# A selective-scan kernel: the state laid out as pairs of states by 64 channels, instead of one state by 128 channels

## The reference, cut to what matters

```python
dt = softplus(dt_low @ dt_proj_w.T + dt_proj_b)        # 256 channels d
def step(h, inputs):                                   # h: 256 channels x 16 states
    dt_t, B_t, C_t, u_t = inputs
    dA = jnp.exp(dt_t[:, :, None] * A)
    h = dA * h + (dt_t * u_t)[:, :, None] * B_t[:, None, :]
    y = jnp.einsum('bdn,bn->bd', h, C_t)
    return (h, y)
```

## Time and profile before

| | |
|---|---|
| median of 3 runs | 1285.89 us |
| lowest and highest | 1283.64, 1287.60 us |
| the profiled execution | 1284.42 us |
| its span in the trace | 1282.6 us |
| mean granted PE clock | 0.936 of full speed |
| share of the span busy: PE, DVE, ACT, POOL | 84%, 90%, 64%, 86% |
| moved by DMA | 116.78 MB |

### The profile page before, as it was taken

How to read it: one execution, slowest core, us unless ns; L and a number is a source line. 1 busy time by engine, 2 the same in 40 slices (tenths; PEclk the granted TensorE clock), 3 DMA queues, 4 the chain that set the end, 5 groups by cost and what they waited for, 6 DMA issues and landing times.

```text
span 1282.6 us, 13041 instructions
## 1 busy us (share of the span) xinstructions
PE 1072.5 (84%) x3642; PEld 613.6 (48%) x3642; DVE 1150.1 (90%) x1341; ACT 819.0 (64%) x1532; POOL 1106.9 (86%) x747
## 2 busy tenths in 40 slices
PE   5678878888888887888888889888878878888797
PEld 4334545545545544544455455445445445454344
DVE  1299999999999999999999999999999999999782
ACT  2476766766666667757667666666667676576543
POOL 4199898898898898998988988988988989989663
PEclk8699998998998999999999989989999999998898
DMA  6222221221222312212222212222122132222561
GB/s 162 76 76 76 81 100 65 98 100 58 99 76 86 101 57 105 100 57 98 87 77 80 101 57 99 93 71 99 59 102 101 57 105 100 74 99 87 181 206 37
DMA packets 64538, 116.78 MB, mean 91 GB/s; under 512 B 34218, under 2 KB 47954, under 8 KB 64466
## 3 DMA queue, kind: packets, MB, share of 16 engines
q1 hardware_dynamic: 64466, 115.96, 26.9%
HBM read 108.47 MB, written 7.47 MB: 90 GB/s over the span
## 4 chain that ended last, share of the span: by engine, by line
POOL 27%; DVE 24%; issue 21%; PE 19%; ACT 7%; POOLq 0%; DMA 0%; DVEq 0%; SPq 0%; ACTq 0%
POOL SCAN L414 15%; DVE SCAN L984 15%; PE Yp L711 7%; POOL SCAN L426 6%; DVE SCAN L939 5%; PE PP L740 2%; PE PP L862 2%; PE PP L790 2%; PE PP L842 2%; POOL XN L451 2%; PE PP L835 1%; DVE GATES L968 1%; ACT SGZ L599 1%; POOL GATES L419 1%; POOL XN L442 1%
## 5 line engine op out<-in xcount | busy, mean ns | idle before, releaser
L984 DVE TENSOR_TENSOR_SCAN SCAN<-DA,CAR,SCAN 128x384 f32<-128x384 f32 x768 | 729.8, 1000 | 39.3 <-POOL SCAN L426 35.7
L414 POOL TENSOR_TENSOR SCAN<-SCAN,CS 128x768 f32<-128x768 f32 x384 | 692.3, 1817 | 23.1 <-DVE SCAN L984 18.9
L711 PE MATMUL Yp<-SCAN,IDENT 128*128 128x384 f32 x1536 | 592.6, 511 | 101.1 <-POOL SCAN L414 93.0
L491 ACT ACTIVATE DA<-UDT,A 128x384 f32<-128x384 f32 x768 | 441.6, 581 | 365.3 <-DVE SCAN L984 362.5
L711 PEld LDWEIGHTS Yp<-SCAN,IDENT 128*128 128x128 f32 x1536 | 288.8, 198 | 309.8 <-POOL SCAN L414 147.3
L939 DVE TENSOR_TENSOR SCAN<-UDT,BB 128x768 f32<-128x768 f32 x288 | 268.4, 932 | 11.1 <-PE BB L693 9.2
L426 POOL TENSOR_TENSOR SCAN<-UDT,BS 128x768 f32<-128x768 f32 x96 | 174.4, 1817 | 0.0
L862 PE MATMUL PP<-XN,WT 128*128 128x384 f32 x384 | 140.4, 501 | 0.0
L446 POOL TENSOR_TENSOR UDT<-UDT 128x768 f32<-128x768 f32 x24 | 43.5, 1811 | 69.9 <-DVE UDT L1068 69.9
L862 PEld LDWEIGHTS PP<-XN,WT 128*128 128x128 f32 x384 | 75.6, 199 | 56.7 <-issue 11.7
L693 PE MATMUL BB<-PT,SEL 96*128 96x384 bf16 x288 | 97.7, 340 | 4.1 <-DVE SCAN L939 4.1
(11 more groups left out here) (167 smaller groups left out, 1090.2 us busy)
## 6 DMA issues: line engine op xcount, KB each, us to landing
CS<-bc_rows SPq DMA_DIRECT2D x96, 768.0 KB, 4.1
BS<-bc_rows SPq DMA_DIRECT2D x24, 768.0 KB, 6.0
out<-XN SPq DMA_DIRECT2D x32, 192.0 KB, 2.5
X<-in_x SPq DMA_DIRECT2D x24, 192.0 KB, 3.5
X<-in_L_ffn_memory_tokens SPq DMA_DIRECT2D x16, 256.0 KB, 3.0
XN<-in_L_ffn_memory_tokens SPq DMA_DIRECT2D x16, 256.0 KB, 3.3
bc_rows<-XDT SPq DMA_DIRECT2D x24, 48.0 KB, 1.5
X<-in_L_ffn_memory_router SPq DMA_DIRECT2D x1, 512.0 KB, 4.0
```

The costliest lines, as they stand in the source:

```text
L414: pool.tensor_tensor(M[:, n1 % MRING], HB[:, n1 % HRING], over_halves(CS[:, n1 % CRING]), ALU.mult).then_inc(m_ready, 1)
L491: act.activation(DA[:, h, 0:T], DT[:, par, h], ACT.Exp, scale=A[:, h, n:n + 1])\
L711: last = pe.matmul(Yp[:, h, 0:T], IDENT[:, :], M[:, n3 % MRING, h], start=n3 == 0, stop=n3 == NS - 1)
L984: dve.tensor_tensor_scan(HB[:, s % HRING, h], DA[:, h, 0:T], HB[:, s % HRING, h], CAR[:, ds(J * NS * HALVES + s * HALVES + h, 1)], ALU.mul ...
```

## The change

- The state is laid out with two states on the partitions: partition i * 64 + d holds state i * 8 + j of channel d of a group of 64. Step n of the 16 does pair j = n // 2 and channel half n % 2, with the half's two groups of 64 channels where the two halves stood. Shapes and counts of scans and products stay.
- For this dt and dt*u are needed in the new layout. They are computed as before, in a single buffer `DTN` (no longer one for each parity), and four DMAs copy them into `D4` (`spread_dt`): each source half of 64 partitions to both destination halves. SP issues them between the last C rows of the unit and the next unit's B. ACT's decay, DVE's and POOL's drives wait for `d4_loaded`.
- A row pair of B, spread by PE, serves two steps: 8 matmuls a unit instead of 12, into one buffer instead of two, at even steps and behind the sum over n. C is loaded once for two steps, half of the bytes; C and B for POOL come in two DMAs of 64 partitions each.
- The sum over n is a matmul with a 128 x 64 matrix `STK` (two identities stacked) for each group of 64 channels, the two on two 64-column groups of PE.
- Softplus two steps sooner: PE's matmul for dt at step 5, ACT at 6, 7, 8 and 10, POOL at 9, DVE at 11; POOL's dt*u at 12 instead of 13, and there ahead of the second norm. B and C have their own PSUM bank `XP`.
- The token's dt*u goes through four small DMAs before the first state is set; A's logarithm is loaded in two pieces.

Cut to its core:

```diff
-HRING, MRING, CRING = 8, 4, 8
+HRING, MRING, CRING = 8, 4, 4
+HP = P // 2
+PAIRS = NS // 2
...
-        U, DT, DTU = (UDTv[:, k] for k in range(3))
+        U = sb("U", [P, 2 * HALVES * T])[:, :].rearrange("p (r h t) -> p r h t", r=2, h=HALVES)
+        DTN = sb("DTN", [P, 2 * HALVES * T])
+        DT, DTU = (DTN[:, k * HALVES * T:(k + 1) * HALVES * T].rearrange("p (h t) -> p h t", h=HALVES)
+                   for k in range(2))
+        D4 = sb("D4", [P, 8 * HALVES * T])[:, :].rearrange("p (r k h g t) -> p r k h g t", r=2, k=2, h=HALVES, g=2)
...
-        BB = ctx.enter_context(nc.psum_tensor("BB", [P, 2, 512], F32))
+        BB = ctx.enter_context(nc.psum_tensor("BB", [P, 512], F32))
+        XP = ctx.enter_context(nc.psum_tensor("XP", [P, 512], F32))
...
             def load_c(unit, p, gi):
 
                 positive(sp, m_ready, NS * unit + GRP * (gi - 1))
-                rows = ROWS_D[p, NS + gi * GRP:NS + gi * GRP + GRP]
-                sp.dma_start(CS[:, (gi % 2) * GRP:(gi % 2) * GRP + GRP],
-                             rows.unsqueeze(0).broadcast_to([P, GRP, T])).then_inc(c_loaded[gi % 2], 16)
+                for i in range(2):
+                    rows = ROWS_D[p, NS + i * PAIRS + 2 * gi:NS + i * PAIRS + 2 * gi + 2]
+                    sp.dma_start(CS[i * HP:(i + 1) * HP, (gi % 2) * 2:(gi % 2) * 2 + 2],
+                                 rows.unsqueeze(0).broadcast_to([HP, 2, T])).then_inc(c_loaded[gi % 2], 16)
...
+            def spread_dt(f, p):
+
+                sp.wait_ge(dtu_ready, f + 1)
+                positive(sp, scan_done, 2 * NS * (f - 1))
+                for g in range(2):
+                    for i in range(2):
+                        sp.dma_start(D4[i * HP:(i + 1) * HP, p, :, :, g].rearrange("p k h t -> p (k h) t"),
+                                     DTN[g * HP:(g + 1) * HP, :].rearrange("p (c t) -> p c t", t=T))\
+                            .then_inc(d4_loaded, 16)
...
                 load_c(J, par, 2)
                 load_c(J, par, 3)
                 if front:
+                    spread_dt(J + 1, 1 - par)
                     load_b(J + 1, 1 - par)
                     load_c(J + 1, 1 - par, 0)
...
                     pool.tensor_tensor(M[:, n1 % MRING], HB[:, n1 % HRING],
-                                       over_halves(CS[:, n1 % CRING]), ALU.mult).then_inc(m_ready, 1)
+                                       over_halves(CS[:, n1 // 2 % CRING]), ALU.mult).then_inc(m_ready, 1)
...
-                if front and s == 11:
+                if front and s == 9:
 
                     pool.wait_ge(sq_e_ready, f + 1)
                     pool.tensor_tensor(SE[:, :, :], SE[:, :, :], SR[:, :, :], ALU.mult).then_inc(cr_ready, 1)
...
+                if front and s == 12:
+                    pool.wait_ge(dt_ready, f + 1)
+                    positive(pool, d4_loaded, 64 * f)
+                    pool.tensor_tensor(DTU, DT, U[:, fp], ALU.mult).then_inc(dtu_ready, 1)
                 if back and s == 13:
...
-                if front and s == 13:
-                    pool.wait_ge(dt_ready, f + 1)
-                    pool.tensor_tensor(DTU[:, fp], DT[:, fp], U[:, fp], ALU.mult).then_inc(dtu_ready, 1)
...
-                act.activation(DA[:, h, 0:T], DT[:, par, h], ACT.Exp, scale=A[:, h, n:n + 1])\
+                act.activation(DA[:, h, 0:T], D4[:, par, 0, n % 2, h], ACT.Exp,
+                               scale=A[:, n % 2 * 2 + h, n // 2:n // 2 + 1])\
...
                         if n1 == 0:
-                            act.wait_ge(dt_ready, unit + 1)
+                            act.wait_ge(d4_loaded, 64 * (unit + 1))
...
-                if front and s == 8:
+                if front and s == 6:
 
                     act.wait_ge(dtp_ready, f + 1)
...
-            def spread_b(unit, par, n):
-
-                before = NDVE * unit + dve_index(n)
-                positive(pe, dbu_dve, before - 1)
-                pe.matmul(BB[:, dve_index(n) % 2, 0:T], SEL[:, n], PT[:, par], start=True, stop=True)\
-                    .then_inc(b_ready, 1)
+            def spread_b(unit, par, pair):
+
+                positive(pe, dbu_dve, NDVE * unit + dve_index(2 * pair))
+                pe.matmul(BB[:, 0:T], SEL[:, pair], PT[:, par], start=True, stop=True).then_inc(b_ready, 1)
...
-                if main:
-                    if s + 2 < NS and s + 2 not in POOL_STATES:
-                        spread_b(J, par, s + 2)
-                    elif s + 2 >= NS and front:
-                        spread_b(J + 1, 1 - par, s + 2 - NS)
...
-                    for h in range(HALVES):
-                        last = pe.matmul(Yp[:, h, 0:T], IDENT[:, :], M[:, n3 % MRING, h],
-                                         start=n3 == 0, stop=n3 == NS - 1)
+                    for c in range(2):
+                        last = pe.matmul(Yp[c * HP:(c + 1) * HP, n3 % 2, 0:T], STK[:, :], M[:, n3 % MRING, c],
+                                         start=n3 < 2, stop=n3 >= NS - 2, tile_position=(0, c * HP))
                     last.then_inc(ysum_done, 1)
+                if main and s % 2 == 0:
+                    if s + 2 < NS:
+                        spread_b(J, par, s // 2 + 1)
+                    elif front:
+                        spread_b(J + 1, 1 - par, 0)
...
-                if front and s == 7:
+                if front and s == 5:
 
                     pe.wait_ge(hi_ready, f + 1)
                     if back:
                         pe.wait_ge(x2_ready, k + 1)
                     for h in range(HALVES):
-                        if h == 1:
-                            pe.wait_ge(parts_ready, f + 1)
                         last = pe.matmul(PP[:, h, 0:T], DTW[DTROW:XROWS + 1, h], XDT[DTROW:XROWS + 1, :],
                                          start=True, stop=True, tile_position=(DTROW, 0))
...
-                dve.wait_ge(b_ready, NDVE * unit + dve_index(n) + 1)
-                dve.tensor_tensor(HB[:, n % HRING], DTU[:, par], over_halves(BB[:, dve_index(n) % 2, 0:T]), ALU.mult)\
+                dve.wait_ge(b_ready, PAIRS * unit + n // 2 + 1)
+                dve.tensor_tensor(HB[:, n % HRING], D4[:, par, 1, n % 2], over_halves(BB[:, 0:T]), ALU.mult)\
                     .then_inc(dbu_dve, 1)
...
                     elif s + 1 == NS and front:
-                        dve.wait_ge(dtu_ready, J + 2)
+                        dve.wait_ge(d4_loaded, 64 * (J + 2))
                         drive(J + 1, 1 - par, 0, N + 1)
...
-                if front and s == 13:
+                if front and s == 11:
 
                     dve.wait_ge(r2_ready, 2 * f + 1)
...
-                if front and s == 13:
+                if front and s == 11:
                     dve.wait_ge(r2_ready, 2 * f + 2)
...
             def first_main():
-                dve.wait_ge(dtu_ready, 1)
+                dve.wait_ge(d4_loaded, 64)
                 drive(0, 0, 0, 0)
```

More of the change, by code:

```diff
@@ L337, in _ @@
             load_c(0, 0, 0)
+            spread_dt(0, 0)
+            sp.wait_ge(set_dve, 10)
+            for g in range(2):
+                for i in range(2):
+                    sp.dma_start(TDU4[i * HP:(i + 1) * HP, g:2 * HALVES:2], TDU[g * HP:(g + 1) * HP],
+                                 allow_slow_non_contiguous=True).then_inc(tdu4_loaded, 16)
             spread(0, 0)
@@ L591, in step @@
                         .then_inc(sp_chain, 1)
-                if front and s == 10:
+                if front and s == 8:
                     act.wait_ge(sp_chain, 3 * f + 3)
@@ L739, in step @@
                     for h in range(HALVES):
-                        last = pe.matmul(PP[0:XROWS, 1, 0:T], XPT[:, h], U[:, fp, h], start=h == 0, stop=h == 1)
+                        last = pe.matmul(XP[0:XROWS, 0:T], XPT[:, h], U[:, fp, h], start=h == 0, stop=h == 1)
                     last.then_inc(xp_ready, 1)
@@ L870, in step @@
                     pe.wait_ge(hi_ready, f + 1)
-                    pe.matmul(PP[0:DTROW, 1, 0:T], LESS[:, 0], PART[:, :], start=False, stop=False,
+                    pe.matmul(XP[0:DTROW, 0:T], LESS[:, 0], PART[:, :], start=False, stop=False,
                               skip_group_check=True).then_inc(res_ready, 1)
@@ L1012, in step @@
                     dve.tensor_tensor(TDU, TDT, TU, ALU.mult).then_inc(set_dve, 1)
-                    dve.wait_ge(set_dve, 10)
-                    for h in range(HALVES):
-                        last = dve.tensor_scalar(CAR[:, 0:NS * HALVES].rearrange("p (n h) -> p n h", h=HALVES)
-                                                 [:, :, h], DA[:, 0, 16:32], TDU[:, h:h + 1], None, ALU.mult)
+                if at(J, -1) and s == 15:
+                    dve.wait_ge(tdu4_loaded, 64)
+                    for i in range(2):
+                        for c in range(2 * HALVES):
+                            last = dve.tensor_scalar(
+                                CAR[i * HP:(i + 1) * HP, c:NS * HALVES:2 * HALVES],
```

(2 more changed lines are left out.)

73 lines of the change are left out of this document (40 added, 33 removed).

## The result

The changed kernel takes 1448.06 us (median of 4 runs, 1447.78 to 1450.05), against 1286.09 us of the kernel before beside it (4 runs, 1283.64 to 1287.60). The ratio is 1.1265, 95% interval 1.1244 to 1.1285: 12.6% slower. I had forecast 1353 us and a range up to 1402. The sign was right, the size was not: +162 us where I had +69.

What follows compares the result with a forecast made beforehand. DVE was taken to set the pace, POOL close behind and PE hidden. 1284.4 us plus 60 for the loop (+2.6 us, 23 times) plus 9 at the start gave 1353 us; 1284 to 1402 held some 0.8.

Steps and rivals of the forecast that it cites:

- POOL's lag: POOL enters a unit late after waiting 2.77 us for softplus; DVE's resulting 1.77 us of waits were to go.
- The holds: Softplus on DVE: L968 and L1068 held by POOL's products, locks costing 2.9 us a unit against 1.54 before.
- Slower, at 0.83: Whole kernel: chance 0.83 of slower, against 0.13 faster and 0.04 same.
- The start, +9: Ahead of the first drive(0): 8.65 us of copies, some 2 us of small ones, up to 1.7 saved; +9 us.
- matmul of dt ahead of B: PE, step 5: dt's matmul ahead of B for states 8 and 9 makes DVE lose 1.0 us at drive(8).
- L1068 ahead of POOL's clamp: Last softplus operation on DVE slips in between POOL's product 11 and its clamp, ending at 41.8 us.
- copies 8.6 us: Four copies of dt and dt*u land 8.6 us after dt*u, the middle of 6.4 and 10.9.
- The end, net 0: Kernel's end: perhaps 3 us gained from PE's shorter sum, as much lost by gathers queued on SP; net 0.
- +2.6: Loop: a unit of 52.25 us against 49.68, 23 times, +60 us.
- Rival 3: Copies take 10.9 us: unit 54.55 us, 1407 us in all; chance 0.11, shared with another wait.
- Rival 4: PE's relief matters, as PE is busy 42.67 of 49.3 us; put at under 3 us, no chance given.
- DVE's own work of 46.4 us a unit: DVE's unit of 49.68 us less 1.77 of waits and 1.54 of hold; none of the 46.4 goes.

Runs made afterwards that it cites:

- sum_wide: Changed kernel with the sum over n done again by 128-column matmuls, zeros in the other 64 columns: 1482.69 us.
- split_pe_busy: split with eight more matmuls, whose result nobody reads, in PE's idle time at step 12: 1372.85 us.
- spread_first: Changed kernel with PE's matmul of B for states 8 and 9 ahead of dt's matmul: 1421.53 us.
- mended version: Changed kernel with dt copied before dt*u, two PSUM buffers for B, B of state 8 ahead of dt's matmul, dt*u ahead of POOL's clamp: 1346.46 us.
- before_m1_behind: Kernel before, with its first softplus product on DVE (L968) moved from ahead of scan 13 to behind it: 1290.88 us, ratio 1.0064.
- split: Changed kernel with dt copied as soon as it is there and dt*u after its product, eight transfers of 192 KB: 1379.3 us.
- d4_whole: Changed kernel with dt and dt*u copied in two transfers of all 128 partitions, half of the channels getting the wrong dt: 1388.53 us.

## Why the prediction was right and wrong

**What was right.** DVE set the pace, through a wait at drive(0) for the copies, once a unit. POOL's lag and the waits for its B products went (35.7 us to none). The holds came where the text put them and at nearly the length that it gave: L998 1.94 for 1.85 us, L1102 2.37 for 2.7. Slower, at 0.83, was right. The start, +9, was measured as +9.0, but by luck: dt*u ended at 57.00 us where it had ended at 61.07, 4.1 us earlier and not 1.7, and from there to drive(0) it took 13.1 us and not 10.65, since the token's small copies, issued behind the four large ones, landed only at 68.3.

**Where it failed.** The prediction's unit was 52.25 us; the one shown is 736.45 - 680.92 = 55.53. By its own steps, counted from drive(0) at 680.92:

| step | predicted | measured | more |
|---|---|---|---|
| B of state 8 there | 22.6 | 704.55 - 680.92 = 23.6 | 1.0 |
| dt ready (end of L1102) | 41.8 | 723.83 - 680.92 = 42.9 | 1.1 |
| end of dt*u | 43.6 | 726.29 - 680.92 = 45.4 | 1.8 |
| copies landed | 52.25 | 55.5 | 3.3 |

- The term **matmul of dt ahead of B**: 1.0 us, measured 1.80 at drive(8) and 0.34 at drive(6). The order was right, but the sum for state 3 was costed at 0.75 us and B at 0.33, at the full clock. They took 1.37 and 0.50, at 0.74 and 0.50 of it. That makes 0.6 us, and the wait at drive(6), which had no term, most of the rest. It carries 1.0 us into dt. I had dismissed PE since it waited little and had less to do; that its matmuls might run at the lower clock was nowhere in the sum. What keeps the clock low at this place isn't settled: more work on PE raised the mean clock (sum_wide 0.864, split_pe_busy 0.874), but in sum_wide this place was at half the clock all the same.
- The choice **L1068 ahead of POOL's clamp**: DVE's operation (now L1102) did run ahead, but the clamp stood behind it and ahead of dt*u. Once POOL's product 11 was over the clamp was started, held behind L1102, and dt*u came behind both. The prediction had dt*u begin right at dt's end; it began 0.7 us after it.
- The term **copies 8.6 us**, the middle of 6.4 and 10.9: measured 10.1. It was a mean between two mechanisms, transfers between halves at the full rate or at half of it, and the lower rate is the one near which they ran: 181 to 222 GB/s against 366 with all partitions. The upper bound, 0.8 us too high, was nearer. The Trainium skill (SBUF — State Buffer, The DMA port swizzle) gives about 218 GB/s for 64 partitions, and says (same page, "Can I just issue two DMAs to hit both halves?") that two transfers to the two halves don't add up. The trace agrees, with 220 and 222 GB/s in the windows. The estimate of 9.2 us from that page was nearer than my 8.6, and still 0.9 short.
- **The end, net 0**: +5. The last unit's gate product waits 12.27 us for PE, against 7.68 before, though the wait of the last gate product, 9.01 us, is shorter than the 10.12 of the kernel before.

So the failed steps of the prediction are three terms of one chain, dt's way to drive(0), each sized too small (PE's matmuls, the clamp, the copies), and the end.

The sum: the mean unit is 55.8 us, 3.5 above the 52.25 of the prediction. The "+2.6" was taken against one unit of 49.68 us, where the mean is 49.3; against that the growth is 6.5, so the loop was 3.9 x 23 = 90 us too short, and the end 5: 1353 + 90 + 5 = 1448 us.

**Rival 3** (copies of 10.9 us, 1407 us) was the nearest, for half of its reason: the copies are 1.5 of the 3.3 us in the table. **Rival 4** said that PE's relief gives under 3 us. No run tests that, and it was asked in one direction only: that PE could become late was no rival, and spread_first puts 26.5 us on its order alone. That DVE waits for PE "twice in the whole trace" was also misread: the trace of the kernel before has 24.8 us in 3 times at L964 and 9.2 in 3 at L939 besides, though of these only 0.4 us lie in the steady loop. The range's upper end, 1402, lay below even rival 3's 1407, and had no room for the delays of PE and POOL on top of it.

**A number that the runs put in place.** DVE's own work of 46.4 us a unit is right as work: the mended version's terms add up with it. But the 1.54 us of hold taken off to get it weren't there for the taking: before_m1_behind shows them covering ACT's squares, and with ACT's order changed too some 13 us came back, of 24 x 1.4 = 34.

What stays open: what PE's clock is worth in the 63 us of the mended version, since no run has both a full clock and the mended order. Nor was there a run with PE's waits taken away whole and the copies left as they are, so account B has no bound of its own.

## What to carry to other kernels

Cost a new transfer by the partitions that it reads and writes, not by its bytes, and don't cost the engine in front of it at the full clock when the change adds waits to it. When a wait is removed, look for the second-latest arrival at the same instruction: here copies and B are both late at drive(0), so each mend alone gave 27 to 69 us of the 166 us of waits. And an operation that lasts longer than it should may be covering another engine's lateness; move both together.

## What the runs showed of the hardware

- Transfers from SBUF to SBUF with 64 partitions at each end: 181 to 222 GB/s for four in flight together, at a busy share of 0.94 to 1.03. Eight of half the size (split): 240. With 128 partitions (d4_whole): 366 GB/s. An issue of such a copy took 1.27 us of SP's queue (four in 5.06 us), against 0.32 us for a load of C from DRAM.
- Two 128 x 64 float32 matmuls on the two column groups took 0.87 us together, four instructions, where two 128 x 128 took 1.46.
- The granted clock was 0.50 after the 7.5 us of idle time on PE, in both units shown (the changed kernel and split), and stayed at 1.0 where matmuls filled all but 2.2 us of that time (split_pe_busy). The statistics took 3.8 us at the one and 2.1 at the other.
- The exclusion of DVE and POOL holds a POOL operation with one input too: the clamp, begun while DVE's L1102 ran, lasted 1.53 us and not 0.83.
